# Transposes of the two normalised activations moved from TensorE to DMA, in a program written out straight

## The reference, cut to what matters

```
x = x + tanh(g_xattn) * xattn(layernorm(x), token_ids, ctx, ctx, ctx)
x = x + tanh(g_ffn)  * ffn(layernorm(x), Wr, br, Wd, bd, Wu, bu)
xattn: e = min(token_id // 6250, 3)
       y = (silu(h @ Wg[e].T) * (h @ Wu[e].T)) @ Wd[e].T      # Wg = Wu = Wd = ctx
ffn:   w = softmax weights of the best 2 of 8 experts, from h2 @ Wr + br
       out = sum_e w[e] * (relu(h2 @ Wd[e] + bd[e]) @ Wu[e] + bu[e])
```

## Time and profile before

| | |
|---|---|
| median of 3 executions | 203.82 us (203.39 to 203.85) |
| span of the profiled execution, first to last instruction | 201.4 us |
| what the median has beyond that span | 2.4 us |
| busy: PE, DVE, ACT, POOL | 175.0, 155.7, 111.9, 99.7 us |
| chain that ended last | PE 44%, issue 18%, POOL 10%, DVE 9%, DMA 7%, ACT 4% |
| DMA traffic | 13.43 MB, mean 67 GB/s |

### The profile page before, as it was taken

How to read it: one execution, slowest core, us unless ns; L and a number is a source line. 1 busy time by engine, 2 the same in 40 slices (tenths; PEclk the granted TensorE clock), 3 DMA queues, 4 the chain that set the end, 5 groups by cost and what they waited for, 6 DMA issues and landing times.

```text
span 201.4 us, 4382 instructions
## 1 busy us (share of the span) xinstructions
PE 175.0 (87%) x1074; PEld 104.0 (52%) x1075; DVE 155.7 (77%) x523; ACT 111.9 (56%) x224; POOL 99.7 (50%) x246
## 2 busy tenths in 40 slices
PE   1576896999997989999999999999999999976560
PEld 1564463655553656656656556655665655534310
DVE  4859696697768799889888998797877878678640
ACT  2596599884287166473665726547265561545200
POOL 4478846427246366375553735516244162445641
PEclk9999999999999999999999999999999999999955
DMA  5947572101210201203101011011010100101121
GB/s 135 370 163 231 205 216 69 52 5 20 86 55 0 52 0 52 59 0 104 55 0 54 0 52 52 2 52 52 0 54 0 52 20 33 52 0 55 52 104 52
DMA packets 6784, 13.43 MB, mean 67 GB/s; under 512 B 2392, under 2 KB 2520, under 8 KB 6768
## 3 DMA queue, kind: packets, MB, share of 16 engines
q0 software_dynamic: 2560, 8.39, 12.6%
q1 hardware_dynamic: 4208, 4.86, 7.3%
HBM read 9.06 MB, written 4.19 MB: 66 GB/s over the span
## 4 chain that ended last, share of the span: by engine, by line
PE 44%; issue 18%; POOL 10%; DVE 9%; DMA 7%; ACT 4%; DVEq 3%; SPq 2%; POOLq 1%; ACTq 0%
PE ps_y L603 6%; PE ps_y L605 6%; PE ps_y L604 6%; PE ps_a L603 4%; PE ps_a L605 4%; PE ps_a L604 4%; DMA xs<-in_x_dram,rows_of 4%; ACT h L796 3%; POOL rs L457 3%; PE ps_h2T L685 2%; PE ps_pT L624 2%; DMA bu_nat<-in_L_ffn_bu_dram 2%; POOL hot_slot L432 2%; PE ps_hT L677 2%; POOL xs L439 2%
## 5 line engine op out<-in xcount | busy, mean ns | idle before, releaser
L456 POOL TENSOR_SCALAR ve<-mv 128x1 f32<-128x1 f32 x32 | 7.7, 239 | 62.6 <-DVE mv L1099 51.8
L796 ACT ACTIVATE h<-xs,mrs,rs 128x512 f32<-128x512 f32 (+1 forms) x16 | 21.1, 1317 | 22.4 <-POOL mrs L458 22.4
L783 ACT ACTIVATE pT_hi<-ps_pT 128x512 f16<-128x512 f32 x19 | 11.3, 595 | 36.0 <-PE ps_pT L624 36.0
L603 PE MATMUL ps_y<-w_hi,pT_hi 128*128 x76 | 28.8, 379 | 2.3 <-DVE w_lo L952 1.5
L603 PE MATMUL ps_a<-w_hi,hT_hi 128*128 x76 | 29.1, 382 | 0.7 <-DVE hT_lo L1074 0.6
L604 PE MATMUL ps_a<-w_lo,hT_hi 128*128 x76 | 29.1, 382 | 0.0
L605 PE MATMUL ps_a<-w_hi,hT_lo 128*128 x76 | 29.0, 381 | 0.0
L604 PE MATMUL ps_y<-w_lo,pT_hi 128*128 x76 | 28.8, 379 | 0.0
L605 PE MATMUL ps_y<-w_hi,pT_lo 128*128 x76 | 28.8, 379 | 0.0
L1086 DVE SCALAR_TENSOR_TENSOR xs<-ps_y,y_t,xs 128x512 f32 x19 | 14.3, 750 | 10.2 <-PE ps_y L605 7.7
L529 POOL DMA_INDIRECT out_dram<-xs,rows_of x16 | 17.3, 1083 | 5.9 <-DVE xs L1117 3.5
(11 more groups left out here) (209 smaller groups left out, 424.0 us busy)
## 6 DMA issues: line engine op xcount, KB each, us to landing
w_nat<-in_ctx_dram SPq DMA_DIRECT2D x4, 1024.0 KB, 7.9
xs<-in_x_dram,rows_of POOLq DMA_INDIRECT x16, 3.6
wd_nat<-in_L_ffn_Wd_dram SPq DMA_DIRECT2D x1, 256.0 KB
wu_nat<-in_L_ffn_Wu_dram SPq DMA_DIRECT2D x1, 256.0 KB
out_dram<-xs,rows_of POOLq DMA_INDIRECT x16, 2.9
b_in<-in_L_ffn_bd_dram SPq DMA_DIRECT2D x1, 64.0 KB
bu_nat<-in_L_ffn_bu_dram SPq DMA_DIRECT2D x3, 16.0 KB
tok_i<-in_itok_BxS_dram SPq DMA_DIRECT2D x1, 8.0 KB, 1.8
```

The source lines that it names most:

```text
L603: mm(ps[:, :], lhs_hi[:, kc, :], hi, start=(kc == 0), stop=False)
L796: a(h2[:, :, :], x1[:, col(k), :].rearrange("p o (q c) -> p c (o q)", c=KC), ACT.Identity, bias=mrs[:, 1, col(k)], scale=rs[:, 1, col(k)]) ...
```

## The change

Three edits belong together.

1. The rows of `h` and `h2` are split before they are transposed: ACT copies the fp32 rows to fp16 (`h_parts[:, 0, :]`), DVE subtracts that copy and writes the rest (`h_parts[:, 1, :]`), both in SBUF. One DMA from SP, `dma_start_transpose`, then turns 128 rows of 1024 fp16 numbers (256 KB) into eight blocks of 128x128, `hT[k % 2]` or `h2T[k % 2]`. Only pair 0 keeps the way over PE. There are 18 such DMAs for pairs 1 to 18 and 16 for tiles 0 to 15, all in SP's queue, each behind waits. The first stands ahead of the eight small loads.
2. The buffers are doubled, with waits for the DMA that read a buffer or the product that used it.
3. The hardware loops, the `gate` writes and the counter `x_in` go away; every step is written out.

```
 def transpose_h(k):                                    # new, on SP
     sp.wait_ge(h_lo_done, k)
     wait_last(sp, a_done, k - 1)
     sp.dma_start_transpose(hT[k % 2], h_parts[k % 2]).then_inc(s_hT[k - 1], 16)
...
                 if t == AHEAD - 1:
+                    transpose_h(1)
                     sp.dma_start(b_in[:, 0:ER], ...)
...
+            for i in range(1, T + LATE + 2):
+                if i + 1 < NP:
+                    transpose_h(i + 1)
+                if some(T, -2 - LATE, i):
+                    k = i - 2 - LATE
+                    sp.wait_ge(h2_lo_done, k + 1)
+                    if k > 1:
+                        sp.wait_ge(hid_mm, k - 1)
+                    sp.dma_start_transpose(h2T[k % 2], h2_parts[k % 2]).then_inc(s_h2T[k], 16)
...
             def hidden_product(k):                     # PE
-                pe.wait_ge(h2T_lo_done, k + 1)
+                pe.wait_ge(s_h2T[k], 16)
...
-                if some(NP, 1, i0):                    # PE, step
+                if i == -1:
                     for c in range(KC):
                         last = tr(ps_hT[:, c, :], h[:, c * P:(c + 1) * P], ident[:, :])
-                if some(T, -2 - LATE, i0):
-                    for c in range(KC):
-                        last = tr(ps_h2T[:, c, :], h2[:, c, :], ident[:, :])
...
                     a(h2[:, :, :], x1[...], ACT.Identity, ...).then_inc(normed2, 1)   # ACT, step
+                    a(h2_parts[k % 2][:, 0, :], h2[...], ACT.Copy).then_inc(h2_hi_done, 1)
...
+                    a(h_parts[k % 2][:, 0, :], h[:, :], ACT.Copy).then_inc(h_hi_done, 1)
...
+            def h_low(k):                              # DVE
+                dve.wait_ge(h_hi_done, k)
+                v.tensor_tensor(h_parts[k % 2][:, 1, :], h[:, :], h_parts[k % 2][:, 0, :],
+                                ALU.subtract).then_inc(h_lo_done, 1)
```

More of the change, by code:

```diff
@@ L188, in bass_flamingo_gated_kernel @@
         h = sb("h", [P, D])
-        hT_hi = sb("hT_hi", [P, KC, P], fp16)
-        hT_lo = sb("hT_lo", [P, KC, P], fp16)
+        h_parts = [sb(f"h_parts{b}", [P, 2, D], fp16) for b in range(2)]
+        hT = [sb(f"hT{b}", [P, 2, KC, P], fp16) for b in range(2)]
         silu = sb("silu", [P, D])
@@ L195, in bass_flamingo_gated_kernel @@
         h2 = sb("h2", [P, KC, P])
-        h2T_hi = sb("h2T_hi", [P, KC, P], fp16)
-        h2T_lo = sb("h2T_lo", [P, KC, P], fp16)
+        h2_parts = [sb(f"h2_parts{b}", [P, 2, D], fp16) for b in range(2)]
+        h2T = [sb(f"h2T{b}", [P, 2, KC, P], fp16) for b in range(2)]
         hid = sb("hid", [P, HC])
@@ L272, in bass_flamingo_gated_kernel @@
         hT_lo_done = sem("hT_lo_done")
+        h_hi_done = sem("h_hi_done")
+        h_lo_done = sem("h_lo_done")
+        s_hT = [sem(f"s_hT{k}") for k in range(1, NP)]
         a_done = sem("a_done")
@@ L285, in bass_flamingo_gated_kernel @@
         normed2 = sem("normed2")
-        h2T_done = sem("h2T_done")
-        h2T_hi_done = sem("h2T_hi_done")
-        h2T_lo_done = sem("h2T_lo_done")
+        h2_hi_done = sem("h2_hi_done")
+        h2_lo_done = sem("h2_lo_done")
+        s_h2T = [sem(f"s_h2T{k}") for k in range(T)]
         hid_mm = sem("hid_mm")
@@ L311, in some, with pipeline @@
             return 0 <= i + off < n
[L313 to L334, removed]
+        def pipeline(step, first, pairs, tiles):
+            for i in range(first, max(NP - min(pairs), T - min(tiles))):
+                step(i, i)
         def col(k):
@@ L342, in wait_last @@
         def wait_last(eng, done, k):
-            if not (isinstance(k, int) and k == 0):
+            if k:
                 eng.wait_ge(done, k)
@@ L387, in _ @@
             load_weights(2)
-            for t in range(T):
+            for t in range(AHEAD):
                 sp.wait_ge(s_gather[t], 16)
-                sp.sem_inc(x_in, 1)
                 if t == 0:
@@ L664, in step @@
                     k = i
[L665 removed]
+                    if i < E:
                         wait_low(pe, i)
[L667 to L668 removed]
+                    if k == 0:
+                        pe.wait_ge(hT_lo_done, 1)
+                    else:
+                        pe.wait_ge(s_hT[k - 1], 16)
+                    wait_last(pe, prod_done, k)
+                    split_product(ps_a, hT[k % 2][:, 0, :, :], hT[k % 2][:, 1, :, :],
+                                  e_now).then_inc(a_done, 1)
                 if some(T, -4 - LATE, i0) and has_a:
@@ L1152, in step @@
                                     ALU.subtract).then_inc(wtT_lo_done, 1)
+                if some(NP, 1, i0):
+                    h_low(i + 1)
                 if some(NP, -1, i0) and not ending:
@@ L1209, in _ @@
             top_rows(2)
-            hT_low(0)
+            hT_low_0()
             top_row(2)
```

97 lines of the change are left out of this document (47 added, 50 removed).

## The result

The changed kernel takes 256.44 us (median of 4 executions, 254.92 to 256.95) against 203.83 us (203.39 to 203.88) on the same chip: ratio 1.2576, interval 1.2535 to 1.2617. The forecast was 245 us in a range from 215 to 300. The profiled execution spans 255.0 us; its device time of 256.79 lies 1.8 us above that.

The account below looks back on a forecast made before the run. PE was taken to bound the kernel before, a step's dependent chain with the DMA (P = 10.3) after. Terms summed to +41.9 on a 201.4 us span, 243.3; with 2.4 more about 245.7, stated as 245, range 215 to 300.

Parts of the forecast that it names:

- P >= 6.1 + D: Full step's length P: hidden product through low part of h2, 6.1 us, then D, before the next hidden product; 10.3 us.
- a clock row below 1.00 in the middle: Sign that the prediction is wrong: PE's granted clock falls below 1.00 in the middle of the changed kernel.
- D = 4.2: Second layer: time from the low part's end until PE may read h2T, 4.2 us; likely band 2.4 to 6.1.
- 6.1 us for PE's, ACT's and DVE's part of the loop: One full step: hidden 0.71, pT 0.44, `ps_a` 2.75, silu to `prod` 0.81, to low part 0.67, low part 0.68.
- the clock as a rival: Full steps: at 1.2 GHz PE's 3.9 us in the loop double, +47 us over 12 steps, about 292 us; chance 0.10.
- Small loads +6.9: Start: loads stand behind the first transposing DMA, 6.2 us late, plus 0.7 for DVE's h_low(2) ahead of pT_lo.
- Steps 1 to 5, -1.3: Early short steps: three groups of transposes leave a PE that has no gap there, saving 1.3 us.
- The end, +9.9: After the full steps: tile 13's hidden product ahead of the last `ps_y`, +1.6, and the drain, +8.3 us.
- First layer hidden unless D > 4.4: First layer's transposes hidden behind 6.1 us of PE work even in steps 1 to 5; shown only above D = 4.4.
- PE's saving is gone: Full steps at P = 10.3, 1.9 us more than before: PE waits 3 us a step.
- Loop B 1.0 us shorter: Two-step loop, 2P >= 15.3 + D: must be 1.0 us shorter than its rows for P under 7.55.
- the rival where PE stays the bound: Faster: both loops shorter than summed, steps of 7.3 us, 201 us or 194 if small loads hide; chance 0.05.

Follow-up runs that it names:

- low_early: The changed kernel with DVE's low part of h2 moved right behind pT_lo and the statistics, ahead of the weights and `prod`: 231.36 us, ratio 1.143.
- loads_first: The changed kernel with the first transposing DMA moved behind the eight small loads in SP's queue: 253.82 us, ratio 1.249 against the kernel before.
- straight_only: The kernel before, written out without loops, gate writes and the x_in counter, all transposes on PE: 201.22 us, ratio 0.991.
- second_layer_dma: The changed kernel with the first layer's transposes back on PE and the small loads early again: 245.17 us, ratio 1.207 against the kernel before.
- scatter_later: The changed kernel with POOL's scatter of a tile issued behind its square root of the same step: 254.19 us, ratio 1.252 against the kernel before.

## Why the prediction was right

The direction, the loop that sets the step and the order of the terms held; the forecast was 11 us low, and errors of both signs stand behind that number. By its steps:

- **What bounds it.** "P >= 6.1 + D" is confirmed by the rows of a step and by low_early, which shortened just that loop and took 25 us off. The prediction's own sign against it, a clock row below 1.00 in the middle, did come, beside the loop and not in its place.
- **D = 4.2, from the small loads' row.** Over the 12 steps it was 3.79 (3.12 to 4.48); 3.1 undisturbed. -0.4 us a step.
- **6.1 us for PE's, ACT's and DVE's part of the loop** is the term that was mis-sized. It is 6.31 in an undisturbed step (9.45 less 3.14) and 7.29 in the mean. Of the 0.2 us between 6.1 and 6.31 most is the hand-over from `ps_a` to silu, 0.33 us, for which the sum had nothing. The difference to the mean over 12 steps is 11.7 us: 9.4 in the six steps in which `ps_a` ran partly at the lower clock, 2.3 in three more in which `prod` stood 0.75 us behind DVE's statistics. DVE would have held `prod` in the first four of the six as well; by an estimate from these numbers DVE is then worth 5.2 us (seven steps of 0.75) and the clock alone 6.5. The forecast had the clock as a rival that doubles every step or none; it came in part, in about every second step. With +2.5 for the 6.31 and -4.9 for D the steps cost 31.7 us against 22.4.
- **Small loads +6.9**: +6.7, in part by luck. SP held the first transposing DMA for 1.34 us and not 0.6, but the loads then landed sooner: from the first issue to `router_bias` 7.31 us, where it was 8.19. But "undo it and it comes back", the reading behind loads_first, failed: two waits ended close to each other.
- **Written-out steps**, counted as nothing: straight_only took 2.1 us off.
- **Steps 1 to 5, -1.3**: the pT transposes of step 5 start at 66.36 instead of 58.19. Of these 8.2 us 6.7 are the loads; 1.7 more went when `ps_y` of pair 0 ran at the lower clock, and 0.2 was gained, not 1.3. From there to the first hidden product +4.5, forecast +4.0.
- **The end, +9.9** (tile 13 and drain): +9.3.
- **First layer hidden unless D > 4.4**: right after pair 1, which waited 2.88 us; one more wait has 0.2 us.
- **"PE's saving is gone"** with its 3 us of waiting a step: 42.3 us for 16 tiles, 2.6 each.
- **"Loop B 1.0 us shorter"**, in the rival where PE stays the bound: by the prediction's own sums loop B over its two steps would have to be 2.0 us shorter, and loop A 0.4 us too.

The Trainium skill ("VectorE: DVE Perf Modes", the three transpose paths) gave the rival estimate of 10.5 us for eight blocks one after another; the trace disagrees, with 3.1 and 3.7 us (the medians of the two layers) from issue to landing. Its 261 GB/s ("DMA: Bandwidth & Descriptors", latency table) is nearer: the halved transfer saved 0.6 us for 128 KB, an estimated 220 GB/s, beside the estimated 1.9 us that do not depend on size.

Open remains why D is 4.1 to 4.6 in some steps with no gather or scatter issued near. In second_layer_dma and scatter_later such a long D and a D near 3.1 follow each other in turn, tile by tile, at the end of the full steps.

## What to carry to other kernels

Moving work off the busiest engine paid here only outside the loop that sets the step: the same DMA saved 0.3 us a step in the first layer, where its operand is ready long before, and cost 2.6 in the second, where the next hidden product waits for it. Before sending a hand-over through a DMA, sum the dependent chain of one step with the transfer's whole time in it (here 3.1 us at best, 3.8 in the mean), and issue its last input as early as the engine's order allows. A wait put into a full TensorE can be paid twice, as here in about every second step: once as idle time and again as slower matmuls behind it.

## What the runs showed that was not expected

- SP's rows show 1.19 to 1.24 us for most issues of a transposing DMA, 128 KB or 256 KB alike, against 0.56 for a small plain load; that is 40% of D at its shortest.
- A 256 KB transpose within SBUF adds about 1050 packets (42693 instead of 6784 for 34 of them).
- PE's matmuls of 128x512 ran 0.43 us apart behind waits of 3.67, 3.78, 3.95 and 2.82 us, at full clock behind 1.98, 1.87, 1.85 and 1.57. Waits of 3.56 (the row below) and 2.87 cost nothing and one of 2.01 did, so the wait alone does not decide:

```profile
90.90 0.23 PE L635 MATMUL ps_hid<-w_in_hi,h2T 128*128 128x136 f16 x1 [3.56 <-DMA h2T<-h_parts]
```

- Hardware loops and the writes ahead of waiting instructions together cost about 2 us in this kernel: steps of 8.29 to 8.71 us became an even 8.29 after the first.
